# AdaLN and ternary ffn over 128 samples: the ffn weight is loaded behind the first weights, and the first second products follow in pairs

## What is computed

```
a = einsum('bsd,bdh->bsh', x, W[cat]) + b[cat][:, None, :]
w_scale = mean(abs(weight)) + EPS
w_quant = clip(round(weight / w_scale), -1, 1)
a_scale = max(abs(a), axis=-1) + EPS
a_quant = round(clip(a / a_scale * 127, -128, 127))
y = einsum('bsi,oi->bso', a_quant, w_quant) * (w_scale * a_scale / 127)
out = x + y
```

## Time and profile before

| what | value |
|---|---|
| median of three runs | 500.86 us (498.65, 500.86, 501.11) |
| the profiled execution's own time | 498.48 us |
| its span in the trace | 496.5 us |
| TensorE busy (matmuls) | 488.1 us of the span, 98% |
| GpSimd, VectorE, ScalarE busy | 381.9, 355.3, 335.3 us |
| moved by DMA | 172.69 MB, 348 GB/s in the mean |

### The profile page before, as it was taken

One profiled execution on the slowest core, in us unless ns is written; L12 is line 12 of the kernel. 1 busy time (PEld: TensorE's weight loads), 2 busy tenths in 40 slices (PEclk: granted clock), 3 DMA queues, 4 the chain that ended last, 5 costly groups with the idle time before them and its releaser, 6 DMA issues.

```text
span 496.5 us, 13136 instructions
## 1 busy us (share of the span) xinstructions
PE 488.1 (98%) x2178; PEld 360.5 (73%) x2226; DVE 355.3 (72%) x654; ACT 335.3 (68%) x502; POOL 381.9 (77%) x399
## 2 busy tenths in 40 slices
PE   8999999999999999999999999999999999999997
PEld 3667777777777777777777777777777777777774
DVE  6758776587866796877766869855978587566854
ACT  3676856677668677768656597766877667567642
POOL 8579787687976897988776979866988688676850
PEclk9999999999999999999999999999999999999999
DMA  7889997999999999999999999999999999799943
GB/s 238 278 274 409 413 335 270 322 411 398 353 324 398 358 415 408 411 406 409 340 318 354 307 402 412 406 331 347 413 411 402 339 401 330 245 365 335 326 155 142
DMA packets 71730, 172.69 MB, mean 348 GB/s; under 512 B 8097, under 2 KB 8354, under 8 KB 71586
## 3 DMA queue, kind: packets, MB, share of 16 engines
q1 hardware_dynamic: 53714, 139.88, 76.3%
q10 hardware_dynamic: 18000, 32.64, 17.9%
HBM read 138.94 MB, written 33.55 MB: 347 GB/s over the span
## 4 chain that ended last, share of the span: by engine, by line
PE 93%; issue 1%; ACT 0%; DVE 0%; ACTq 0%; DVEq 0%
PE ps_cond L761 23%; PE ps_cond L759 23%; PE ps_cond L760 23%; PE ps_y L708 21%; PE ps_aT L719 3%; PE ps_cond L708 0%; ACT ps_cond L413 0%; ACTq L404 0%; ACT sb_aT L479 0%; DVE sb_x_rows L613 0%; DVE sb_x_rows L658 0%; DVEq L43 0%; ACT sb_a_rounded L497 0%; ACTq L413 0%; ACTq L490 0%
## 5 line engine op out<-in xcount | busy, mean ns | idle before, releaser
L363 POOL TENSOR_TENSOR sb_xT_lo<-sb_xT_raw,sb_xT_hi 128x512 fp32r<-128x512 f32 x128 | 167.3, 1307 | 95.0 <-PE ps_cond L761 89.4
L759 PE MATMUL ps_cond<-sb_w_hi,sb_xT_hi 128*128 (+1 forms) x512 | 225.3, 440 | 0.7 <-POOL sb_xT_lo L363 0.7
L761 PE MATMUL ps_cond<-sb_w_hi,sb_xT_lo 128*128 (+1 forms) x512 | 201.4, 393 | 0.0
L760 PE MATMUL ps_cond<-sb_w_lo,sb_xT_hi 128*128 (+1 forms) x512 | 199.4, 389 | 0.0
L627 DVE TENSOR_REDUCE sb_absmax<-ps_cond 128x1 f32<-128x512 f32 x128 | 87.6, 685 | 86.3 <-PE ps_cond L761 84.7
L380 POOL TENSOR_SCALAR sb_y_scale<-sb_absmax,sb_w_step 128x1 f32<-128x1 f32 x128 | 139.2, 1088 | 6.5 <-DVE sb_absmax L627 6.5
L413 ACT ACTIVATE ps_cond<-sb_w_raw 128x512 f32 x127 | 75.6, 595 | 92.0 <-issue 63.2
L582 DVE TENSOR_TENSOR sb_w_lo<-sb_w_raw,sb_w_hi x106 | 126.4, 1231 | 8.9 <-issue 8.3
L708 PE MATMUL ps_y<-sb_ffnT,sb_aT 128*128 128x512 bf16 x458 | 119.1, 378 | 2.8 <-ACT sb_aT L479 0.3
L759 PEld LDWEIGHTS ps_cond<-sb_w_hi,sb_xT_hi 128*128 128x128 f32 x512 | 96.4, 188 | 31.2 <-issue 1.0
L497 ACT ACTIVATE sb_a_rounded<-ps_cond,sb_a_inv 128x512 int8<-128x512 f32 x128 | 87.7, 685 | 45.2 <-DVE sb_a_inv L633 44.5
(11 more groups left out here) (90 smaller groups left out, 52.8 us busy)
## 6 DMA issues: line engine op xcount, KB each, us to landing
sb_w_raw<-cond_wb SPq DMA_DIRECT2D x53, 768.0 KB, 7.7
sb_xT_raw<-x_t SPq DMA_DIRECT2D x128, 256.0 KB, 5.7
sb_x_rows<-x SPq DMA_DIRECT2D x128, 256.0 KB, 5.8
out<-sb_x_rows ACTq DMA_DIRECT2D x124, 256.0 KB, 5.6
sb_w_raw<-cond_wb SPq DMA_DIRECT2D x53, 512.0 KB, 5.8
sb_w_raw<-cond_wb SPq DMA_DIRECT2D x5, 256.0 KB, 4.0
sb_ffn_raw<-ffn_t SPq DMA_DIRECT2D x1, 1024.0 KB, 7.5
out<-sb_x_rows SPq DMA_DIRECT2D x3, 256.0 KB, 2.1
```

Of the source, the lines that this page charges most:

```text
L363: pool.tensor_tensor(xT_lo[:, m, :], xT_raw[:, m, :], xT_hi[:, m, :].bitcast(F32), ALU.subtract).then_inc(x_lo_done, 1)
L759: pe.matmul(ps_cond, x_hi_k, w_hi_k, start=(start and k == 0), stop=False, skip_group_check=True)
L760: pe.matmul(ps_cond, x_hi_k, w_lo_k, start=False, stop=False, skip_group_check=True)
L761: last_mm = pe.matmul(ps_cond, x_lo_k, w_hi_k, start=False, stop=(k == KD - 1), skip_group_check=True)
```

## The change

Seven things are changed, all in the first eight steps:

1. SyncE issues the x load of step 4 together with those of steps 2 and 3, ahead of the weights; before, it came behind the weight of step 4.
2. The ffn weight and the first rows are loaded behind the weights of steps 1 to 5, no longer ahead of the x loads.
3. TensorE's sum for the ternary weight moves from ahead of step 2 to the inside of step 4, ahead of its last three matmuls.
4. VectorE makes the ternary weight in step 3 (both passes), not in steps 0 and 1.
5. Second products 0 and 1 come behind step 5, 2 and 3 behind step 6, in place of one each behind steps 3 to 6. The results on VectorE and the stores on ScalarE follow in the same pairs.
6. The multiplications of zeros in the first steps are gone.
7. ScalarE rounds step 0 right behind the weight branch of step 1, moves the transposes of steps 0 and 1 one step sooner, and takes the ffn weight's sum of absolute values in step 2, behind that step's rounding.

```diff
-    BUSY, BUSY_BEHIND, BUSY_FIRST = 20, 4, 3
+    FFN_STEP, Y_FIRST = 4, 5
+    BUSY, BUSY_BEHIND = 20, 4
...
+        def first_second_products(u):
+            return range(2 * (u - Y_FIRST), min(2 * (u - Y_FIRST) + 2, u - Y_BEHIND + 1)) if u >= Y_FIRST else range(0)
...
-            sp.dma_start(ffn_raw[:, :], ffn_t[:, :]).then_inc(ffn_loaded, 16)
-            sp.dma_start(x_rows[:, 0, :], x[0, :, :]).then_inc(rows_loaded[0], 16)
...
-            for step in range(2, XT_RING):
-                load_xT(xT_of(step + W_AHEAD - XT_AHEAD), step)
+            for step in range(2, XT_RING + 1):
+                if step == XT_RING:
+                    sp.wait_ge(x_lo_done, 1)
+                load_xT(xT_of(step + W_AHEAD - XT_AHEAD), step % XT_RING)
...
-                if ahead >= XT_RING:
+                if ahead > XT_RING:
...
+            sp.dma_start(ffn_raw[:, :], ffn_t[:, :]).then_inc(ffn_loaded, 16)
+            sp.dma_start(x_rows[:, 0, :], x[0, :, :]).then_inc(rows_loaded[0], 16)
...
-            act.wait_ge(ffn_loaded, 16)
-            act.activation(ffn_abs[:, :], ffn_raw[:, :], ACT.Abs,
-                           accum_out=ffn_sum[:, 0:1]).then_inc(ffn_summed, 1)
...
                 split_high(new, offset, raw, step, step)
+                if step == 1:
+                    round_off(0, 0)
...
-                if not first or u >= T_BEHIND:
+                if first and u == 0:
+                    round_off(1, 1)
+                elif first and u == 1:
+                    split_high(new, offset, raw, r + HI_AHEAD, (u + HI_AHEAD) % U)
+                    move(0, 0, True)
+                elif not first or u > T_BEHIND + 1:
                     move(r - T_BEHIND, (u - T_BEHIND) % U, first)
...
+                if not first or u > 1:
+                    round_off(r, u)
+                if first and u == T_BEHIND:
+                    move(1, 1, True)
+                    act.wait_ge(ffn_loaded, 16)
+                    act.activation(ffn_abs[:, :], ffn_raw[:, :], ACT.Abs,
+                                   accum_out=ffn_sum[:, 0:1]).then_inc(ffn_summed, 1)
+                if first and u >= STORE_BEHIND:
+                    stores.append(element)
+                    if u > Y_FIRST:
+                        for _ in range(2):
+                            step = u - STORE_BEHIND + 1 - len(stores)
+                            store(stores.pop(0), step, step)
...
-                    ternary_begin()
-                    new, offset, raw = w_raw_slot(dve, LO_AHEAD)
-                elif first and u == 1:
+                    new, offset, raw = w_raw_slot(dve, LO_AHEAD)
+                elif first and u == FFN_STEP - 1:
+                    ternary_begin()
                     ternary_end()
...
-                if not first or u >= Y_BEHIND:
+                if first:
+                    for step in first_second_products(u):
+                        result(step, step)
+                else:
                     result(r - Y_BEHIND, (u - Y_BEHIND) % U)
...
-                    if first and u < T_BEHIND + 2:
-                        busy(y_ps[1], BUSY_FIRST)
                     a_transpose(r - T_BEHIND, (u - T_BEHIND) % U, first)
...
-                    if first and u == Y_BEHIND:
-                        busy(y_ps[1], BUSY_FIRST)
-                    second_product(r - Y_BEHIND, (u - Y_BEHIND) % U, first)
+                if first:
+                    for step in first_second_products(u):
+                        second_product(step, step, True)
+                else:
+                    second_product(r - Y_BEHIND, (u - Y_BEHIND) % U, False)
...
-                    if first and u == 2:
-                        pe.wait_ge(ffn_summed, 1)
-                        pe.wait_ge(consts_done, 9)
-                        pe.matmul(y_ps[0][:, 8:9], ones[:, :], ffn_sum[:, :], start=True, stop=True).then_inc(ffn_sum_mm_done, 1)
...
+                    if first and u == FFN_STEP and k == KD - 1:
+                        pe.wait_ge(ffn_summed, 1)
+                        pe.wait_ge(consts_done, 9)
+                        pe.matmul(y_ps[0][:, 8:9], ones[:, :], ffn_sum[:, :], start=True, stop=True).then_inc(ffn_sum_mm_done, 1)
```

More of the change, by code:

```diff
@@ L463, in _, with round_off @@
             act.wait_ge(act_table_done, 2)
+            def round_off(step, n):
+                act.wait_ge(a_inv_done, step + 1)
+                act.activation(a_rounded[:, n % Q_RING, :], cond_ps[n % COND_BANKS][:, :], ACT.Copy,
+                               scale=a_inv[:, n % STAT_RING:n % STAT_RING + 1]).then_inc(a_rounded_done, 1)
             for step in range(1, HI_AHEAD):
@@ L479, in move @@
                 act.activation(*parts_of_aT(n), ACT.Copy).then_inc(aT_moved, 1)
+            stores = []
             def body(r0, u, first, last):
@@ L495, in body @@
                     act.wait_ge(aT_done, r - Q_RING + 1)
[L496 to L499 removed]
+                if not first or u > 1:
[11 more added lines that the diff above has]
+                            store(stores.pop(0), step, step)
+                elif not first:
                     store(element, r - STORE_BEHIND, (u - STORE_BEHIND) % U)
@@ L504, in body @@
                     act.activation(*parts_of_aT(U - 1), ACT.Copy).then_inc(aT_moved, 1)
-                if not last or u + HI_AHEAD < U:
+                if (not last or u + HI_AHEAD < U) and not (first and u == 1):
                     split_high(new, offset, raw, r + HI_AHEAD, (u + HI_AHEAD) % U)
@@ L691, in _ @@
             rest_of_table()
-            def busy(bank, count):
-                for _ in range(count):
-                    pe.matmul(bank[:, :], zeros[:, 0:P], zeros[:, :], start=True, stop=True)
             def second_product(step, n, first):
```

5 lines of the change are left out of this document (removed).

## The result

The changed kernel takes **501.60 us** in the median of 13 executions (500.83 to 504.28), the kernel before beside it 499.50 (13 executions, 498.38 to 501.90). The ratio is 1.0045, 95% interval 1.0032 to 1.0057: slower by some 2.2 us (2.1 between the medians), just inside the 0.5% taken ahead as no difference. So both intervals exclude a gain. The profiled execution took 500.83 us (span 499.1).

The account below looks back on a forecast made before the run. TensorE, busy 488.1 of 496.5 us, was taken as the bound. New waits 2.6 + 2.8 + 0.7 + 0.3 less 3.3 gave +3.1, taken as +3.2: 502.9 us, the middle between levels 501.7 and 504.1; range 498.5 to 506.0.

Parts of the forecast that it names:

- closed gaps: TensorE's idle time and multiplied zeros ahead of steps 2, 3 and second product 0: at most 3.3 us to gain.
- idle ahead of step 4: TensorE ready at about 22.4, step 4 starting at 25.0 after its weight and the seed of bank 4: 2.6 us idle.
- idle ahead of the sum matmul: Inside step 4, TensorE wants the sum at 27.1 and ScalarE has it at 29.85: 2.8 us idle.
- idle ahead of second product 0: TensorE ready at 34.0, the ternary weight at 34.7: 0.7 us idle.
- x of step 6: No term of its own; only x of step 5 was worked out, with 0.9 us of cover.
- result 2, ahead of second product 4: Result 2 on VectorE stands behind the split of step 9's weight: 0.3 us taken, between 0 and 1.0.
- central step: Sum inside step 4 waits behind round_off 2, the maximum of step 2 and the weight's low part: 2.8 us idle.
- I keep 3.8 and 6.4: Landing times in us of the two pieces of step 4's weight, kept from before; landings at 19.4 and 23.0.
- rival 1: Step 4's weight lands at the price of its bytes, 3.8 us, at 20.4: +1.3 to +1.8 us, 499.8 to 502.7; chance 0.19.
- 2, the gaps closed as meant: First steps: only 0.7 and 0.2 us of new waits remain, -2.4 us, 496.1 to 498.5; chance 0.13.
- 3, the clock: TensorE's granted clock falls to 1.2 GHz for one step's matmuls: +6.0 us, 504.5 to 506.9; chance 0.08.
- 4, x of step 5: x of step 5 late behind the ffn load at 220 GB/s, 1.6 us lost: +4.8 us; chance 0.05.

Follow-up runs that it names:

- e4: Changed kernel with ScalarE's sum of absolute values of the ffn weight ahead of the rounding of step 2 and the move of step 1: 500.84 us, ratio 1.0028.
- e5: Changed kernel with the ffn load and the first rows back ahead of the x loads: 502.22 us, ratio 1.0061.
- e13: Changed kernel timed again without any edit: 501.93 us, ratio 1.0042 to the kernel before.
- e3: Changed kernel with the x load of step 4 behind the branches of steps 1 to 3, still ahead of step 4's weight: 502.06 us, ratio 1.0056.
- e6: Changed kernel with GpSimd's first row scales one step later, from step 4 on: 502.69 us, ratio 1.0064.
- e10: Changed kernel with multiplications of zeros in its two large gaps, four ahead of step 4 and nine ahead of the sum matmul: 503.03 us, ratio 1.0061.
- e9: Changed kernel with the x load of step 4 back behind step 4's weight: 503.02 us, ratio 1.0098.
- e1: Kernel before without its nine multiplications of zeros in the gaps of the first steps: 499.59 us, ratio 1.0008.
- e7: Changed kernel with the ffn load early, its sums ahead of step 4 and ternary passes in steps 1 and 2: 498.65 us, ratio 0.9979 to the kernel before.
- e8: As e7, with the x load of step 4 behind the branches of steps 1 to 3: 500.13 us, ratio 0.9999 to the kernel before.
- e11: As e7, with four multiplications of zeros ahead of step 4: 498.75 us, ratio 0.9978 to the kernel before.
- e12: Kernel before with only the x load of step 4 issued ahead, with those of steps 2 and 3: 500.46 us, ratio 1.0013.

## Why the prediction held, and where it was off

| step of the prediction | forecast | measured |
|---|---|---|
| closed gaps | -3.3 | about -3.5 (-3.46 from step 1 to 4, which holds the wait of step 4, +1.2, and what only moved behind it, second product 0, -0.9, and the sum matmul, -0.24) |
| ahead of step 1 | 0 | +0.46 |
| idle ahead of step 4 | 2.6 | about 1.2 |
| idle ahead of the sum matmul | 2.8 | 2.6 (2.38, and restarting) |
| idle ahead of second product 0 | 0.7 | 0.7 (0.62) |
| x of step 6 | covered | 0.67 |
| result 2, ahead of second product 4 | 0.3 | 0 |
| sum | +3.1 | 5.6 - 3.5 = +2.1 (+2.20 from step 0 to 8) |

The forecast was 502.9 us on the middle level, with slower at 0.50; the result, 501.60, has the same sign and a size of +2.2 in place of +3.2. It lies just inside "no difference", which had 0.37, and not in "slower", which had the larger chance. That the sum came as near as 1 us is in part luck: one term was 1.4 too large, and two that were costed at nothing came to 1.1.

**The central step was right**: TensorE waits inside step 4 for a sum that stands on ScalarE behind rounding 2, and that behind the maximum and the splits of a weight. It came at 28.92, forecast about 29.9; the wait was 2.4 to 2.6, forecast 2.8; e4 (0.57 where only the order is other) and e5 (2.37 with an early transfer) show that it is the order and not the ffn transfer. Second product 0 came at 33.82 (34.7), step 4 at 24.21 (25.0), the comparison at 29.78 (30.7).

**The step that failed in size: "I keep 3.8 and 6.4" for the landing of step 4's weight.** SyncE had no slack, as said: the first piece went out 5.13 us behind step 0's start, before 4.14. But the two pieces stood 0.64 apart, not 0.99, and the second landed after 5.2 us: at 22.0 instead of 23.0. Counted from step 0's start it landed 1.4 us sooner than forecast (10.97 us for 12.38), and that is the mis-sized 1.4 us of idle ahead of step 4. I first took it for a consequence of the ffn load's new place, and the runs don't bear that out: with the ffn load behind the weight the second piece took 5.2, 5.5, 5.0, 5.6, 5.2, 5.0 and 5.7 us (after, e13, e3, e4, e6, e10, e9), with it ahead 6.4, 6.9, 6.4, 5.2, 4.9, 5.5 and 5.1 (before, e1, e5, e7, e8, e11, e12). The place of another load sorts them better. Where x of step 4 is issued behind this piece, while it is under way, it took 6.4, 6.9 and 5.7 us (before, e1, e9); where x of step 4 is issued ahead, 4.9 to 5.6 in ten profiles, and 6.4 in e5. That another load is under way can't be the whole reason: in the changed kernel the ffn load goes out at 18.31, 1.5 us behind the piece. So the 6.4 us held for the order in which they were read and not for the new one, and what sets them stays open. In no run did it come near the estimate of 3.8 us by the fit of the Trainium skill, page "DMA: Bandwidth & Descriptors", section "Anatomy of one DMA", which is for the software path; rival 1's mechanism is out, though its time (499.8 to 502.7) holds the result.

**Two terms were costed at nothing.** Ahead of step 1 I had not followed the x load past the counts that SyncE gives for ScalarE's seeds: seeds 2.57 us behind step 0's start in place of 1.88, +0.46 (e3 gives 2.98 from step 0 to 1 against 3.37). I had written that SyncE has no slack, but had applied it to the weight only. And ahead of step 6 I had looked at x of step 5 alone: GpSimd's four scales, which wait for the ternary step, took 4.00 us beside VectorE's passes and held up x of step 6.

**The rivals.** 2, the gaps closed as meant, needed one of the links not to be there, and they are; e7 shows what it takes (the sum ahead of the weight's work) and that it then gives -1.0 us in the median. 3, the clock, had 0.08 for +6.0: a fall occurs in half of the executions, but at the lower level for some 3 us and mostly covered. It was named with the wrong size: what a low clock costs depends on whether a wait stands behind it (in e1's profile none does, and step 4 to 5 takes 1.56 us more; in e13's two waits of 0.62 and 0.67 do, and 0.2 is left). 4, x of step 5, didn't happen: landed at 27.0, ready at 29.2, wanted at 30.08; in e4 that cover was gone and it cost 0.71.

## What to carry to other kernels

Work that the whole program waits for once (here a sum over a weight) belongs on its engine ahead of the first work that itself waits for a late transfer; moving its load alone left the wait as it was (e5: 2.37 for 2.38 us). An edit that removes one wait is worth only what the next chain lets through (e4: 1.8 us taken, 0.95 won; e6: nothing), so write down what arrives next before counting a gain. A transfer's time read from one row (6.4 us before, 5.2 after) holds for that order and execution: carry it over as a range. And when an issue is moved on a queue, follow everything behind it there, counts for other engines included.
